# Another order of work for a transformer block in sandwich form: a new rule for the time between TensorE steps, finer offsets, weight copies right behind the scales

## What is computed

```python
def _L0_ffn_ref(x, gate_w, up_w, down_w, gate_s, up_s, down_s):
    g = jnp.einsum('th,ih->ti', xf, gate_w) * gate_s      # 256 -> 704
    u = jnp.einsum('th,ih->ti', xf, up_w) * up_s
    hdn = jax.nn.silu(g) * u
    out = jnp.einsum('ti,hi->th', hdn, down_w) * down_s
...
x = x + 0.5 * ffn(_layernorm(x))
x = x + attn(_layernorm(x))      # rope on q and k, causal mask, softmax, Wo
x = x + 0.5 * ffn(_layernorm(x))
```

## Time and profile before

| what | value |
| --- | --- |
| median of 3 runs | 797.54 us |
| the profiled execution | 796.63 us |
| its span, first to last instruction | 794.7 us |
| TensorE busy (matmul) | 772.3 us, 97% |
| VectorE busy | 613.8 us, 77% |
| ScalarE busy | 549.6 us, 69% |
| GpSimd busy | 390.8 us, 49% |
| mean granted TensorE clock | 0.996 |

### The profile page before, as it was taken

How to read it: one execution, slowest core, us unless ns; L and a number is a source line. 1 busy time by engine, 2 the same in 40 slices (tenths; PEclk the granted TensorE clock), 3 DMA queues, 4 the chain that set the end, 5 groups by cost and what they waited for, 6 DMA issues and landing times.

```text
span 794.7 us, 17253 instructions
## 1 busy us (share of the span) xinstructions
PE 772.3 (97%) x6144; PEld 523.4 (66%) x6144; DVE 613.8 (77%) x1267; ACT 549.6 (69%) x1064; POOL 390.8 (49%) x430
## 2 busy tenths in 40 slices
PE   5999999999999999999999999999999999999997
PEld 5888888777555555565554566554555457898886
DVE  5667577799899997997998799988988925465543
ACT  4866675345867877757787867778877997466652
POOL 3887777536425553153282143531322256566554
PEclk9999999999999999999999999999999999999999
DMA  9801353203364575254574563643851210210001
GB/s 335 343 3 46 115 159 111 51 3 83 117 181 147 159 222 152 60 123 137 166 184 142 120 125 124 172 96 89 222 109 53 65 45 18 68 36 28 27 27 55
DMA packets 61089, 89.76 MB, mean 113 GB/s; under 512 B 19788, under 2 KB 24268, under 8 KB 60748
## 3 DMA queue, kind: packets, MB, share of 16 engines
q1 hardware_dynamic: 60860, 88.57, 38.8%
q10 hardware_dynamic: 144, 0.07, 0.0%
HBM read 45.52 MB, written 40.76 MB: 109 GB/s over the span
## 4 chain that ended last, share of the span: by engine, by line
PE 83%; DVE 9%; ACT 3%; issue 2%; POOL 1%; DMA 1%; SPq 0%; DVEq 0%; ACTq 0%
PE psum L1009 18%; PE psum L1118 15%; PE psum L1101 12%; PE psum L977 12%; PE psum L1038 11%; PE psum L1076 10%; DVE NP L1361 4%; PE psum L1086 3%; DVE SH L1361 2%; PE psum L995 2%; ACT PT L1226 1%; DMA RD<-wd 1%; POOL HL_f L1421 1%; PE psum L987 1%; DVE HF_f L1300 1%
## 5 line engine op out<-in xcount | busy, mean ns | idle before, releaser
L1226 ACT ACTIVATE PT<-psum 128x512 f32<-128x512 f32 (+2 forms) x640 | 309.7, 571 | 99.0 <-PE psum L1101 97.6
L1361 DVE TENSOR_REDUCE NP<-psum 128x1 f32<-128x512 f32 (+3 forms) x448 | 260.7, 640 | 21.9 <-PE psum L1086 14.1
L1478 POOL TENSOR_SCALAR_AFFINE_SELECT PT<-PT 128x512 f32<-128x512 f32 x128 | 80.9, 638 | 182.3 <-ACT PT L1226 182.1
L1009 PE MATMUL psum<-XH,WG_f 128*128 128x512 f32 x352 | 142.4, 405 | 1.7 <-issue 1.7
L1118 PE MATMUL psum<-PT,V 128*32 128x512 f32 (+3 forms) x1536 | 143.7, 492 | 0.0
L1101 PE MATMUL psum<-Q,K 50*128 50x512 f32 (+2 forms) x768 | 141.5, 408 | 1.8 <-DVE XL L1266 0.7
L1076 PE MATMUL psum<-K,Q 48*128 48x512 f32 (+2 forms) x768 | 138.2, 386 | 5.0 <-ACT PT L1226 2.6
L1009 PE MATMUL psum<-XL,WG_f 128*128 128x512 f32 x352 | 139.1, 395 | 0.0
L1421 POOL TENSOR_TENSOR HL_f<-HF_f,HH_f 128x512 fp32r<-128x512 f32 x80 | 103.2, 1299 | 71.3 <-ACT HH_f L1190 71.0
L1361 DVE TENSOR_REDUCE SH<-psum 128x1 f32<-128x512 f32 (+3 forms) x192 | 103.2, 589 | 13.5 <-PE psum L1086 13.0
L1101 PEld LDWEIGHTS psum<-Q,K 50*128 50x128 f32 x768 | 67.2, 184 | 70.1 <-DVE NP L1361 24.4
(11 more groups left out here) (86 smaller groups left out, 1045.1 us busy)
## 6 DMA issues: line engine op xcount, KB each, us to landing
zd<-ZH SPq DMA_DIRECT2D x32, 512.0 KB, 3.9
Q<-zd SPq DMA_DIRECT2D x64, 192.0 KB, 3.8
K<-zd SPq DMA_DIRECT2D x64, 192.0 KB, 4.8
zd<-ZL SPq DMA_DIRECT2D x16, 512.0 KB, 4.9
od<-OS SPq DMA_DIRECT2D x32, 256.0 KB, 2.3
OC<-od SPq DMA_DIRECT2D x32, 128.0 KB, 2.8
SC<-rd_ SPq DMA_DIRECT2D x32, 128.0 KB, 2.9
X<-x SPq DMA_DIRECT2D x7, 512.0 KB, 12.5
```

The lines of the kernel that those rows point to most:

```text
L1009: ins = tn.matmul(bank(*piece), f32(w) if general else w, f32(x) if general else x, start=(kt + m == 0), stop=(kt + m == 2))
L1226: sc.activation(dst, src, ACT.Exp, scale=0.25).then_inc(S["act_exp"], 1)
L1361: ve.tensor_reduce(out=acc, in_=src, axis=AX, op=ALU.max, negate=True).then_inc(S["dve_max"], 1)
L1478: gp_.affine_select(out=pt, in_=pt, compare_op=ALU.is_ge, fill=0.0, base=0, pattern=[[0, 4], [1, P]], channel_multiplier=-1).then_inc(S["p ...
```

## The change

Five things are changed together. The function `between` takes the place of the table MODE_NS: it keeps the last form and whether the step before was already of that form. `settle` offers a TensorE piece that comes after another TensorE piece as soon as that one has begun, since the engine works in order. The constants of the choice (MODE_PLACE, WINDOW, LOAD_PLACE, FORMS, URGE, WARM_SHARE) and the tables PACE and NUDGE are new, and NUDGE has offsets for single score tiles, columns and FFN blocks (FINE). Where one named piece stood for the last of several that must be over, the whole list now stands, and the program waits for the latest of them. The copies of the FFN weights stand right behind the scales in the order of loads, ahead of ds and x1, and the pieces of the check stand ahead of the first XL and the statistics of chunk 1.

```diff
-MODE_PLACE, DMA_RATE, WINDOW = 2.94, 200.0, 107.2
-MODE_NS = {("full", "half"): 170, ("col", "half"): 105, ("half", "full"): 175, ("half", "col"): 117, ("full", "col"): 70, ("col", "full"): 70,
-           ("half", "mask"): 23, ("mask", "half"): 82, ("full", "mask"): 186, ("col", "mask"): 126, ("mask", "full"): 214, ("mask", "col"): 145,
-           ("mask", "mask"): 103}
-RELOAD_NS, LOAD_PLACE = 115, 8.2
+MODE_PLACE, DMA_RATE, WINDOW = 3.5, 200.0, 221.0
+GROUP = {"full": "full", "half": "half", "mask": "half", "col": "col"}
+TURN_NS = {("full", "half"): 86, ("half", "full"): 86, ("half", "col"): 86, ("col", "half"): 25, ("full", "col"): 95, ("col", "full"): 6}
+SECOND_NS, FRESH_NS, MASKED_NS = {"full": 106, "half": 97, "col": 0}, 104, 40
+RELOAD_NS, LOAD_PLACE = 115, 23.4
...
-FORMS = {"full": 7.4, "half": 0.2, "mask": -0.01, "col": 11.5}
+FORMS = {"full": 10.4, "half": 0.38, "mask": -0.03, "col": 11.7}
+
+
+def between(form, to, slack):
+
+    was, ahead = form
+    a, b = GROUP[was], GROUP[to]
+    ns = MASKED_NS * (was == "mask")
+    if a != b:
+        ns += TURN_NS[a, b] + FRESH_NS * (1 - ahead) * (a != "col")
+        ahead = 0
+    else:
+        ns += SECOND_NS[a] * (1 - ahead)
+        ahead = 0 if a == "col" else 1 if was != "mask" or ahead == 1 else 0.25
+    form[:] = to, 0 if slack < RELOAD_NS else ahead
+    return max(ns, min(max(RELOAD_NS - slack, 0), RELOAD_NS))
...
-URGE = {"pe_s": (12.7, 40.6, 14.2, 12.3, 6.4, -11.9, 0), "pe_st": (54.6, 23.7, 9.7, -20.3, 22.4, 53.1, 0)}
+URGE = {"pe_s": (20.2, 62.5, 10.9, -6.9, 82.8, -127.5, 0), "pe_st": (106.5, 47.4, -4.4, -43.6, 226.8, -27.1, 0)}
...
-        "first maxima": (132.395, 77.935, 175.181), "maxima": 1.498, "pv": -0.217,
-        "projection": (23.482, 6.998), "rows": (2.396, 7.651, 1.704),
...
+        "first maxima": (144.628, 101.48, 178.189), "maxima": 0.942, "pv": 15.491, "projection": (31.951, -0.012),
...
+FINE = {"s": "tile", "h": "column", "ffn": "block"}
...
-                           ("rd0", 0.4), ("rd1", 0.4), ("gs", 0), ("us", 0), ("x1", 0.5), ("ds", 0.13), ("x2", 0.5), ("rq", 0.8), ("ro", 0.26), ("x3", 0.5),
+                           ("rd0", 0.4), ("rd1", 0.4), ("gs", 0), ("us", 0), ("ds", 0.13), ("x1", 0.5), ("x2", 0.5), ("rq", 0.8), ("ro", 0.26), ("x3", 0.5),
...
-            if name == "x1":
+            if name == "us":
...
-            add(at, 350, "dve_bn", who, c, i, after=[ready[i // 2 if len(ready) > 1 else 0]] + ([("act_xn",) + st + (3,)] if st else []))
+            add(at, 350, "dve_bn", who, c, i, after=[("dve_flagint",)] * ((who, c) == ("f1", 1)) + [ready[i // 2 if len(ready) > 1 else 0]] + ([("act_xn",) + st + (3,)] if st else []))
...
+        def wait_st(e, gr):
+
+            for piece in in_order(done, st_all(gr)):
+                e.wait_ge(*piece)
```

More of the change, by code:

```diff
@@ L122, in e_units, with st_all @@
     return [(gr, c2, j, u) for j in range(4 * c2 + 4) for u in units_of(c2, j)]
+def st_all(gr):
+    return [("pe_st",) + unit for c2 in range(2) for unit in e_units(gr, c2)]
 def e_skip(c2, j):
@@ L157, in add @@
         assert piece not in self.place, piece
-        self.place[piece], self.ns[piece], self.after[piece] = place + nudged(piece), ns, [x for x in after if x]
+        self.place[piece], self.ns[piece], self.after[piece] = round(place + nudged(piece), 6), ns, [x for x in after if x]
         self.room[piece], self.empties[piece], self.mode[piece], self.bytes[piece] = room, empties, mode, size
@@ L266, in settle @@
                             warms += 1
-                            ns = self.ns[piece] + max(MODE_NS.get((mode[0], self.mode[piece]), 0), RELOAD_NS * (free[e] < now))
-                            mode[0] = self.mode[piece]
+                            ns = self.ns[piece] + between(mode, self.mode[piece], 0 if free[e] < now else RELOAD_NS)
                             spent.append((now, now + self.ns[piece]))
@@ L302, in settle @@
                     self.began[piece] = now
+                    for x in next_ones.get(piece, ()) if e == "PE" else ():
+                        if engine[x] == "PE":
+                            left[x] -= 1
+                            if not left[x]:
+                                offer(x, now)
                     ends.append((end, number[piece], piece))
@@ L331 @@
 DOWN_FIRST = 4
-WARM_SPAN, WARM_SHARE, WARM_COLD = 2700.0, 0.5, 10000.0
+WARM_SPAN, WARM_SHARE, WARM_COLD = 2700.0, 0.54, 10000.0
 BUSY = {"full": 0.92, "half": 0.85, "mask": 0.75, "col": 0.95}
 FILL = {"full": "full", "half": "half", "mask": "half", "col": "half"}
-URGE = {"pe_s": (12.7, 40.6, 14.2, 12.3, 6.4, -11.9, 0), "pe_st": (54.6, 23.7, 9.7, -20.3, 22.4, 53.1, 0)}
+URGE = {"pe_s": (20.2, 62.5, 10.9, -6.9, 82.8, -127.5, 0), "pe_st": (106.5, 47.4, -4.4, -43.6, 226.8, -27.1, 0)}
 QUOTA = {"pe_s": 5, "pe_st": 5}
[L340 to L343, removed]
-        "first maxima": (132.395, 77.935, 175.181), "maxima": 1.498, "pv": -0.217,
-        "projection": (23.482, 6.998), "rows": (2.396, 7.651, 1.704),
-        "column block": 3.384, "down": (12.494, 6.708)}
@@ L347 @@
-NUDGE = {
[L348 to L359, removed]
+PACE = {"ffn 1": 15.723, "ffn 2": 17.032, "heads": 27.401, "first heads": 52.55, "ffn 2 after heads": -22.307,
+        "first q, k, v": (99.444, 188.217, 87.269, 207.31), "q, k, v": (5.1754, 17.4892, 55.3029), "rows ahead": -7.914,
+        "first maxima": (144.628, 101.48, 178.189), "maxima": 0.942, "pv": 15.491, "projection": (31.951, -0.012),
+        "rows": (17.527, 23.156, 1.704), "column block": 4.189, "down": (15.037, 14.119)}
@@ L402, with in_order, gu_all, dn_all @@
           + [("f2", c) for c in range(8)])
+def in_order(done, pieces):
+    return sorted(pieces, key=lambda piece: -done[piece])
+def gu_all(ph, c):
+    return [(kind, ph, c, i) for i in range(NI) for kind in ("pe_g", "pe_u") if (kind, i) != ("pe_g", NI - 1)]
+def dn_all(ph, c):
+    return [("pe_dn", ph, c, pr, 1) for pr in range(2)]
+def pv_all(b):
+    return [("pe_pv", gr, c2, 2 * c2 + 1) for gr in range(NG * b, NG * b + NG) for c2 in range(2)]
 def x_ready(who, c):
@@ L416, in x_users @@
     if who == "a":
-        return [("pe_qk", c // 2, c % 2, w, ab) for w in range(2) for ab in range(2)] + [("pe_v", c // 2, c % 2, 3)]
-    return [("pe_u", int(who[1]), c, NI - 1)]
+        return [("pe_qk", c // 2, c % 2, w, ab) for w in range(2) for ab in range(2)] + [("pe_v", c // 2, c % 2, i) for i in (1, 3)]
+    return gu_all(int(who[1]), c)
 def x_ring(who):
@@ L628, in maxima @@
                     add(key + 0.5, dve_ns(s_width(t, ch) * (2 if u == "a" else 1)), "dve_max", *unit, hh,
-                        after=[("pe_s",) + unit] + ([("dve_nm", gr - 2, 1)] if gr >= 2 else []),
+                        after=[("pe_s",) + unit] + ([("dve_nm", gr - 2, c) for c in range(2)] if gr >= 2 else []),
                         empties=[("pe_s",) + unit + (hh,)])
@@ L917, in wait_ffn1 @@
         def wait_ffn1(e):
-            e.wait_ge("pe_u", 1, 7, NI - 1)
-            e.wait_ge("pe_dn", 1, 7, 1, 1)
+            for piece in in_order(done, gu_all(1, 7) + dn_all(1, 7)):
+                e.wait_ge(*piece)
             for pr in range(2):
@@ L937, in wait_x_rows @@
             was = prior[x_ring(who), (who, c)]
-            for piece in x_users(*was) if was else x_first(who, c):
+            for piece in in_order(done, x_users(*was) if was else x_first(who, c)):
                 e.wait_ge(*piece)
@@ L1354, in vector_program @@
                     if gr >= 2:
-                        e.wait_ge("dve_nm", gr - 2, 1)
+                        for last in in_order(done, [("dve_nm", gr - 2, c) for c in range(2)]):
+                            e.wait_ge(*last)
                     acc = maxima_of(gr, t, ch)[:, hh, :]
```

84 lines of the change are left out of this document (55 added, 29 removed), and 52 rows, old and new, of the table NUDGE.

## The result

| what | before | after |
| --- | --- | --- |
| median, 9 runs each on the same chip | 796.99 us (794.41 to 798.42) | 799.19 us (798.49 to 802.03) |
| ratio | | 1.0032, 95% interval 1.0019 to 1.0045 |
| the profiled execution | 796.63 us | 798.78 us |
| its span | 794.7 us | 796.5 us |
| mean granted TensorE clock | 0.996 | 0.993 |

The page of the kernel after answers to the earlier trace rows, and the busy time by stretch to the earlier trace rows.

A forecast was written before the change was run, and what follows sets the result against it. In the attention it saw TensorE and VectorE close to the limit, with changes of form costing some 49 us. From 796.6, less 7.0, 4 and 1.3, came 784.3; 0.9 more gave 785.2, rounded to 785.0 us, range 776 to 797.5.

The forecast's parts named there:

- part 1: Attention stage, TensorE: 24 merges of whole-array steps at 0.29 us each save 7.0 us; bounds 0 to 11.3 us.
- part 2: Attention stage: earlier scores feed ScalarE and VectorE sooner, waits fall by 4 us; bounds 8 us less, 10 us more.
- the clock: TensorE's granted clock, low at 17.3 to 20.7 us: net change 0, bounds -1.7 and +1.7 us.
- part 3: Kernel start: weight check ahead of other VectorE work and earlier weight copy save 1.3 us; first FFN matmul at about 14.6.
- the fillers: pe_warm matmuls, put only where no step is ready: a few more or less cost nothing.
- The term that I dismissed: Attention stage: ScalarE waits 96.9 us for TensorE's scores, so it was taken to be no limit as such.
- Parts 4 and 5: FFN weight copies put ahead on SP's queue, 0 us; waits added by lists of last readers, 0 us.
- (a): Attention: VectorE is the real limit, saved changes of form become waits for reduces; 794.2 us, chance 0.18.
- (b): Attention: put-off PV steps keep PT's 4 buffers full, one exponential lost per half group; 803.5 us, chance 0.12.
- (c): Attention: gaps belong to the whole-array step itself, merges bring 0 and waits stay; 796.2 us, chance 0.05.

The follow-up runs named there:

- light_two_after: Kernel after with maxima over a quarter of the columns and exponentials over the first 128 columns of each block: 771.20 us, 0.9678 of the kernel before.
- light_two_before: Kernel before with maxima over a quarter of the columns and exponentials over the first 128 columns of each block: 772.37 us, 0.9686 of the unedited kernel before.
- fill_two: Kernel after with two more matmuls in each of fillers 17 to 21 and 49 to 59: 800.01 us, 1.0035 of the kernel before.
- exp_ahead: Kernel after with a one-column Exp ahead of the attention's first exponential, loading its table early: 796.64 us, 0.9999 of the kernel before.
- mend_fill: Kernel after with Exp table ahead, block 1 of chunk 1 by tanh, one more matmul in fillers 17 to 21: 797.90 us, 1.0011 of before.
- light_before: Kernel before with the row maxima taken over a quarter of their columns: 793.98 us, 0.9957 of the unedited kernel before.
- mend: Kernel after with the Exp table loaded ahead and block 1 of chunk 1 by tanh: 794.62 us, 0.9980 of the kernel before.
- tanh_block: Kernel after with the gate of block 1 of chunk 1 computed by tanh instead of silu: 798.58 us, 1.0013 of the kernel before.
- mend_again: Kernel after with Exp table ahead and block 1 of chunk 1 by tanh, the same program measured a second time: 795.60 us, 0.9982 of before.
- silu_behind: Kernel after with one silu of chunk 1 and its split put behind chunk 0's last on ScalarE: 801.18 us, 1.0059 of the kernel before.

## Why the prediction was wrong

In the terms of the prediction's sum: part 1 was −7.0 us and came as −3.5; part 2 was −4 and came as +1.9; the clock was 0 and came as +3.4; part 3 was −1.3 and came as −0.8 at the first FFN matmul. A term put at nothing, the fillers, came as +2.2: ten more of them stand between 16 and 782 us, at 0.22 us each in the plan. The five add up to +3.2 us, by which TensorE's last matmul came later.

**Part 1, fewer changes of form: right mechanism, count wrong.** I forecast 24 merges and fewer than 65 whole-array stretches. The trace of after has 70 where before had 79, 89 column stretches for 90, and 158 half stretches for 165. Over the whole kernel 384 changes became 362; two changes make one interruption, so that is 11 for my 24. The price agrees: 11 x 0.29 = 3.2 us, and what the new function charges over the real sequence of forms fell from 65.2 to 61.7 us, 3.5 less. The function itself describes the gaps well: on those of before its median miss is some 10 ns, that of the old table some 60 ns. That the saving reaches the time isn't shown. The direct test, light_two_after against light_two_before, gives 1.2 us in the medians of four runs each, with an uncertainty of some 2 us. The clock alone can make that difference: a mean of 0.999 against 0.996. In the two profiles the charges fall by 3.5 us, and TensorE's idle time beyond them grows from 21.0 to 23.2 us, although the 1.7 us of clock at 17.9 are gone: what the merges saved was idle time again. The step that failed is "I take a bit over half", 24 merges where 11 came. MODE_PLACE and WINDOW rose, but URGE rose with them and may pull scores in between; that cause was not tested.

**Part 2, waits: wrong sign.** I took 4 us less. The distances of TensorE's starts beyond their work, less what the new function charges, went from 45.5 to 50.8 us between 16 and 782 us. Of these 5.3 us, 3.4 are clock: 10.2 us at the lower level where before had 3.4. The other 1.9 us are as much as 640 to 660 takes. So the step "I take a tenth, 4 us less" failed. The two rows of waits for VectorE's reduces fell by 3.5 us, the way I had said, but the idle time as a whole rose. The step behind it failed too: that the new rule fits the gaps of a trace doesn't make its plan come true, and the new plan was missed by 7.9 us more than the old one.

**The term that I dismissed.** "ScalarE waits 96.9 us for TensorE's scores in that stage, so it is no limit as such." light_two_before shows 21.6 us hanging on its exponentials once the maxima are light. An engine with long idle stretches can still be late each time that it is needed: it waits for scores, and then TensorE waits for the bank. I didn't look at ScalarE's table loads at all, though one at 186.68 stood in the trace of before, hidden by the projections; an order made anew could uncover it. None of my rivals had it. The fillers I dismissed as well ("a few more or less cost nothing"): leaving out the new order's 53 cost 8.6 us, and adding to them in fill_two held the clock and bought nothing.

**The clock, taken as 0 with 1.7 us either way.** The fall at the start vanished as it might (1.7 us gained), and two others came (5.1 us lost): 3.4 us net, twice my bound. Nine runs of after have a median mean clock of 0.993, before 0.998. Within one kernel the time changes by some 0.4 to 0.7 us for each 0.001 of mean clock (lines through nine or more runs of a kernel; exp_ahead: 798.78 at 0.992, 795.33 at 0.998; mend_fill 802.12 at 0.989, 793.17 at 1.000). 0.005 are thus some 2 to 3.5 us: about the 2.2 us by which the kernel got slower. What the order lost beside the clock took back what it had gained.

**Part 3, the start: half right.** The flag was written at 13.58, 0.75 us earlier, and the first FFN matmul came at 15.16 instead of 15.92; I said 14.6. VectorE's and TensorE's timelines of after, beside the earlier trace rows:

```profile
13.58 0.14 DVE L1377 CAST FLAG<-CST 1x1 int32<-1x1 f32 x1
13.65 1.27 DVE L1362 TENSOR_TENSOR XL<-psum,XH 128x512 fp32r<-128x512 f32 x2
```

```profile
15.16 0.47 PE L1103 MATMUL psum<-XH,WG_f 128*128 128x512 f32 x1 [1.16 <-DVE XL L1362]
```

"The two subtracts (0.68 us each) fit under the 1.45 us of the branch" is the step that failed. They end at 14.92, and the matmul starts 0.24 us behind them, so they are what is late next. Together with the clock that no longer falls at 17.2 the order is 2.7 us ahead in work done at 20 us, and holds that until 180. It is lost in the 20 us that follow.

**Parts 4 and 5** came as forecast: x1's transposes run at 21.69 without idle time before them, and there is no wait of note at the lists of readers.

**The rivals.** (a), VectorE as the limit, is refuted by light_before (0.4%) and by the waits for reduces, which fell. (b), slower by exponentials held up behind put-off PV steps, had the right sign and not the mechanism: the loss sits in three places, two of them at table loads, not once per half of a group. (c), merges that bring nothing, came nearest in time (796.2) and is wrong in its reason. The rule of the Trainium skill that I weighed ("TensorE: Matmul & The Clock Gate", section "The mechanism") would have left the merges without gain. The cadence of 0.12 us and the charges of the real sequence speak against its reason; the direct test, which shows no gain that the clock doesn't explain, can't decide it.

**What stays open.** The parts "rule" and "start" were not separated, since any change of input makes another order. Why the clock falls in one execution of mend and not in another at the same place isn't settled. The fall at 552.8 stood in the profiles of after and tanh_block and in none of the three with the table loaded ahead (exp_ahead, mend, mend_again); but silu_behind, without that load ahead, had its second fall at 671.4 instead. So the load may trigger it, and that isn't shown. Nor is it shown what in ScalarE's hold on the banks costs the 21.6 us: that number bounds it, since light_two leaves the work out and not only the lateness, and it was measured with the maxima light as well.

## What to carry to other kernels

When an order is made anew, list the one-off costs that the old order happens to hide (table loads, first uses, a piece named as "the last") and ask of each whether the planner knows it; here a 1.28 us load that nobody modelled, one named piece and the clock took more than the 4.8 planned microseconds. Busy shares and waits didn't tell which engine bounds: halving the work of VectorE, 89% busy in the attention, gave 0.4%, and relieving ScalarE, 76% busy there, on top of it gave 2.7% more. Compare real with planned starts step by step: it points to the 20 us in which a plan fails.

## What the hardware did that I had not expected

In the kernel after, the granted clock fell to 1.2 GHz at 187.6 for 6.8 us and at 552.8 for 3.4 us, both times among half steps of 48 and 50 rows and fillers. The longest idle time of TensorE shown shortly before was 0.99 us at the first place and 0.26 us at the second. Whether it falls differs between executions of one program, by 3.35 us of 793. Leaving the fillers out brought five falls of 6.8 us in the new order and three of 3.4 us in the attention of the old one; more filler at two places brought none before the very end in the one execution profiled, and with more filler at one place, in the mended kernel, the falls stood elsewhere.
